# Attention scores as four 64-row products side by side, and a fifth addition of a head's exponentials on GpSimd

## The chip, the cores and the metric

One core of one Trainium2 chip. The metric is the device time of one execution in microseconds (us), lower is better. Engines are named as in the profile: PE (TensorE matmul), PEld (its weight loads), DVE (VectorE), ACT (ScalarE), POOL (GpSimd), SP (the queue that issues most DMAs).

## The reference

A pre-normed transformer layer in float32 on x of 4 batches, 1024 tokens, 128 features: attention with 16 heads of 64, rotary embedding on the first 32 of each head's 64 dimensions, and a low-rank feed-forward part.

```python
x = x + attn(layernorm(x), Wq, Wkv, Wout, bout)
x = x + ffn(layernorm(x), U1, V1, b1, U2, V2, b2)
# attn, per head:
q, k = rope(q), rope(k)
sim = einsum('bhid,bhjd->bhij', q, k) * 64 ** -0.5
out = einsum('bhij,bhjd->bhid', softmax(sim), v)      # then out @ Wout + bout
# ffn:
gelu((x @ U1) @ V1 + b1) @ U2 @ V2 + b2
```

## The kernel before

**Passes and steps.** The 64 (batch, head) pairs are worked in 16 groups of `GH` = 4 heads. The first and the last group are written out, the 14 between are a loop; a group is one pass of `STEPS` = 32 steps. Step t scores one tile of 128 keys (`kt` = t % 8) of head t // 8 against all 1024 queries, in two halves z of 512. Scores lie transposed in `S`, keys on partitions; `S` has a buffer for even and one for odd steps.

**A step.** PE makes the scores (`pe_scores`), ACT writes their exponentials to one of 8 slots of `PF` (`act_step`), PE multiplies them with V into `O` (`pe_values`; at even steps, for steps t-4 and t-3, in float32, the two halves on two 64-column tiles of PE). Queries and keys are kept as float16 high and low parts. In `QK` the 128 partitions hold two 64-row operands each: `KHL` is key-high over key-low, `QHH` query-high twice, `KMH` a constant over key-high, `QML` the row maxima over query-low, so that two products of 128 rows per half (L376, L377) give all three partial products and the subtracted maximum.

**Maxima.** Before a head is scored, "units" estimate each query's maximum: `pe_unit` (L397) makes a 128 x 1024 block of scores in `M` with 64-row operands, two products on the two row halves of PE, and DVE takes the maximum of each row (`dve_max`, L603). Unit u = t + 12 (`LEAD`) is made at step t. `M` is one buffer, so that unit u waits until DVE has read unit u-1. At even steps the unit comes behind the V products, at odd steps at the very end. ACT scales the eight maxima of a head (`act_max`), a DMA lays them down as a row (`max_over`).

**Tiles.** Other work of PE goes through one PSUM bank `TILE`, one tile after another, each at the step that the tables say, behind the scores: 8 projections of q and k for the next group (`QK_AT`; "rot" for the rotated halves, "pass" for the rest), 4 of V (`V_AT`), the sums of the denominators on 128x32 tiles (`DEN_AT`) and the output projections (`OUT_AT`). A tile waits until the one before has been read (`freed`). A rot tile of step s goes to DVE (two operations), to POOL (`rot_add`, L652 and L655), to ACT (`act_rot`, step s+3) and to POOL again (`rot_low`, L663, step s+4), which leaves the low part in `STAGE`. A pass tile is copied by ACT (L433) and subtracted by DVE (L535).

**Handover.** `hand_over` (L708, L709; 4 DMAs a head) carries q and k from `STAGE` to `QK`. For head 0 of the next group it waits until all four rot_low and pass subtractions of the pass are done (`rot_lo`, `pass_lo`); unit 32, at step 20, waits for it (`handed`).

**Sums.** For the denominators POOL adds the exponentials of two steps into `SA[0]` or `SA[1]` (`pool_sum`, L676): parts 0 to 3 of a head at POOL steps 8h+2, 8h+4, 8h+6, 8h+8. DVE adds these four into `SUM` with three additions (`dve_sum`, L610 at `kt` 7, L613 at `kt` 1 and 3 of the next head). POOL's part 2 waits for the first of them, parts 0 and 1 of the next head for the others. Denominators are inverted (`INVERT_AT`), spread by DMA, and DVE scales the outputs by them (`dve_norm`, L625, `NORM_AT`).

Every engine works its own steps in order; what stands in front on an engine holds up what is behind it.

Of the kernel before, what the change touches and what calls it, by code (L numbers as in the profile page):

```python
# [27 lines left out]
HAND = 4 * 16  # L28
PV_LAG = 4
# [76 lines left out]
def build(nc, x_d, wq_d, wkv_d, wout_d, bout_d, u1_d, v1_d, b1_d, u2_d, v2_d, b2_d, rope_d, ident_d, out_d):  # L106
    with ExitStack() as ctx:
# [38 lines left out]
        HIGH, LOW = {"k": STAGE[:, 1], "q": STAGE[:, 2]}, {"k": STAGE[:, 0], "q": STAGE[:, 3]}  # L146
# [12 lines left out]
        MX = sb("MX", [P, 2, KT], F32)  # L159
        MN = sb("MN", [P, 2, KT], F16)  # L160
# [9 lines left out]
        H = [QK[:, h, :, :].rearrange("p a b -> p (a b)").bitcast(F32) for h in range(2)]  # L170
        QT = QK[:, 3, :, :].rearrange("p a b -> p (a b)").bitcast(F32)
# [69 lines left out]


# [150 lines left out]
        def pe_unit(e, u, place, q, bank):  # L393

            for c in range(2):
                rows, keys = slice(DH * c, DH * c + DH), slice(c * 512, (c + 1) * 512)
                mm = e.matmul(bank[:, keys], QHH[rows, place, q:N:KT], (KHL, KMH)[c][rows, place, keys],  # L397
                              start=True, stop=True)
            mm.then_inc(unit_made, 1)
# [9 lines left out]
        def pe_step(e, it, t):  # L409
            u = t + LEAD  # L410
            if t % 2 == 0:
                for back in (t - PV_LAG, t - PV_LAG + 1):
                    if back >= 0:
                        pe_values(e, it.step(back), it.i * GH + back // KT, back, it.i)
                    elif not it.first:
                        pe_values(e, it.step(back), it.i * GH - 1, back + STEPS, it.i - 1)
                if not (it.last and u >= STEPS):
                    pe_next_unit(e, it, u)
            pe_scores(e, it, t)
            pe_tiles(e, it, t)  # L420
            if t % 2 == 1 and not (it.last and u >= STEPS):
                pe_next_unit(e, it, u)


        def act_tile(e, kind, args, made, g, bank):

            if kind == "proj" and args[2] == "pass":
# [5 lines left out]
                e.activation(HIGH[w][:, 1, c * 512:(c + 1) * 512], bank, ACT.Copy).then_inc(pass_hi, 1)  # L433
# [9 lines left out]
        def act_rot(e, args, g):  # L443
# [7 lines left out]
            e.activation(HIGH[w][:, 0, c * 512:(c + 1) * 512], YR[:, :], ACT.Copy).then_inc(rot_hi, 1)  # L451
# [21 lines left out]
        def act_tiles(e, it, t):  # L473
            for n, kind, args in it.at(t):
# [7 lines left out]
                elif kind == "den":  # L482
                    act_den(e, it.pair(args), made, bank)
# [626 lines left out]
```

## Time and profile before

| | |
|---|---|
| median of 3 runs | 1556.92 us (1556.63 to 1557.19) |
| the profiled execution: time / span | 1557.27 us / 1555.5 us |
| PE busy | 1424.9 us, 92% |
| DVE busy | 1222.0 us, 79% |
| POOL busy | 977.8 us, 63% |
| ACT busy | 778.3 us, 50% |
| PEld busy | 546.8 us, 35% |
| chain of waits that ended last | PE 56%, DVE 13%, issue 13%, POOL 7%, DMA 5% |
| granted TensorE clock, mean | 0.986 |

The span is the profiler's, from the first to the last instruction; the execution's own time is 1.8 us more. Busy times are sums over the instructions of an engine, matmuls that run side by side counted once. Clock is the share of full speed that PE was granted. In the timelines a line stands for consecutive instructions of one kind: it gives their start, their length together and, in brackets, the idle time before and what ended it. A matmul's line reaches to its modelled end, so the next one can start before it.

### The profile page before, as it was taken

To read this page: it belongs to the slowest core of one execution; us is meant where nothing else is said; L and a number is where in the kernel's file an instruction comes from. 1 tells how busy PE (TensorE), PEld (TensorE's weight loads), DVE (VectorE), ACT (ScalarE), POOL (GpSimd) and SP (SyncE) were. 2 spreads that over 40 slices of the span, in tenths; PEclk is the share of its full clock that TensorE was granted. 3 is DMA by queue.
4 is the path that set the end of the run, shared out by engine and by line. 5 is a ranking of instruction groups with operands and counts; after the bars stand their busy time and mean duration, and the time that the engine had idled before them with its cause. 6 is when DMAs were issued, how large, how long until landed. Compare 5 with 4: busy or idle time off the path is not lost.

```text
span 1555.5 us, 25971 instructions
## 1 busy us (share of the span) xinstructions
PE 1424.9 (92%) x7289; PEld 546.8 (35%) x7289; DVE 1222.0 (79%) x1297; ACT 778.3 (50%) x1512; POOL 977.8 (63%) x501
## 2 busy tenths in 40 slices
PE   3689999999999999999999999999999999998886
PEld 1224333333333333333333333333333333333323
DVE  7787888788788878878788888878887887888744
ACT  3244554545454545555455454545545554544464
POOL 4388766658475665838476574848566584757731
PEclk9799999999999999999999999999999999999999
DMA  5312131221303121120313122031312204031002
GB/s 158 73 26 60 25 76 26 50 54 26 83 14 75 34 57 38 44 65 14 75 34 74 22 54 54 14 79 30 75 21 54 54 20 89 14 75 33 3 15 68
DMA packets 70209, 76.00 MB, mean 49 GB/s; under 512 B 27204, under 2 KB 36936, under 8 KB 69928
## 3 DMA queue, kind: packets, MB, share of 16 engines
q1 hardware_dynamic: 68736, 74.69, 21.4%
q10 hardware_dynamic: 1448, 1.00, 0.3%
q8 instruction: 13, 0.21, 0.1%
q14 instruction: 12, 0.10, 0.0%
HBM read 22.56 MB, written 2.36 MB: 16 GB/s over the span
## 4 chain that ended last, share of the span: by engine, by line
PE 56%; DVE 13%; issue 13%; POOL 7%; DMA 5%; ACT 3%; SPq 2%; DVEq 0%; ACTq 0%; POOLq 0%
PE O L388 18%; PE S L376 10%; PE S L377 8%; PE M L397 8%; DVE MX L603 5%; PE TILE L312 5%; DVE SUM L613 4%; DMA QK<-STAGE 4%; POOL SA L676 3%; PE TILE L322 2%; POOL STAGE L663 2%; ACT PF L515 2%; SPq L708 1%; PE TILE L306 1%; PE TILE L330 1%
## 5 line engine op out<-in xcount | busy, mean ns | idle before, releaser
L676 POOL TENSOR_TENSOR SA<-PF 128x1024 f32<-128x1024 f32 x256 | 616.5, 2424 | 372.5 <-DVE SUM L610 279.9
L515 ACT ACTIVATE PF<-S 128x512 f32<-128x512 f32 x1024 | 547.8, 599 | 564.9 <-PE S L377 564.1
L603 DVE TENSOR_REDUCE MX<-M 128x1 f32<-128x1024 f32 x504 | 614.5, 1219 | 229.3 <-PE M L397 229.1
L388 PE MATMUL O<-PF,V 128*64 128x512 f32 x2048 | 497.4, 607 | 0.0
L376 PE MATMUL S<-QK 128*128 128x512 f16 x1024 | 393.1, 384 | 0.0
L377 PE MATMUL S<-QK 128*128 128x512 f16 x1024 | 390.1, 381 | 0.0
L397 PE MATMUL M<-QK 64*128 64x512 f16 x1008 | 221.9, 437 | 65.9 <-DVE MX L603 47.7
L613 DVE TENSOR_TENSOR SUM<-SUM,SA 128x1024 f32<-128x1024 f32 x128 | 248.3, 1939 | 3.6 <-POOL SA L676 3.4
L397 PEld LDWEIGHTS M<-QK 64*128 64x128 f16 x1008 | 72.6, 140 | 370.8 <-DVE MX L603 247.9
L388 PEld LDWEIGHTS O<-PF,V 128*64 128x64 f32 x2048 | 124.5, 136 | 206.4 <-issue 149.8
L376 PEld LDWEIGHTS S<-QK 128*128 128x128 f16 x1024 | 99.9, 98 | 165.3 <-issue 64.2
L652 POOL TENSOR_TENSOR T<-T,ROPE 128x512 f32<-128x512 f32 x60 | 76.3, 1271 | 127.8 <-DVE T L532 127.8
L494 ACT ACTIVATE OS<-O 64x512 f32<-64x512 f32 x128 | 75.8, 592 | 130.8 <-PE O L388 130.0
L377 PEld LDWEIGHTS S<-QK 128*128 128x128 f16 x1024 | 100.7, 98 | 76.8 <-issue 1.4
L655 POOL TENSOR_TENSOR YR<-T 128x512 f32<-128x512 f32 x60 | 113.1, 1886 | 4.7
L663 POOL TENSOR_TENSOR STAGE<-YR,STAGE 128x512 f16<-128x512 f32 x64 | 97.7, 1526 | 21.1 <-ACT STAGE L451 21.1
L312 PE MATMUL TILE<-XT,WQK 128*128 (+1 forms) x372 | 102.4, 385 | 6.3 <-ACT V L441 2.6
L610 DVE TENSOR_TENSOR SUM<-SA 128x1024 f32<-128x1024 f32 x64 | 81.8, 1278 | 19.8 <-ACT DS L471 19.8
L330 PE MATMUL TILE<-WO,OS 128*128 (+1 forms) x504 | 68.9, 280 | 16.9 <-DVE OS L625 14.7
L625 DVE TENSOR_TENSOR OS<-OS,RB 128x1024 f32<-128x1024 f32 x32 | 78.7, 2460 | 6.4 <-DMA RB<-den 6.4
L330 PEld LDWEIGHTS TILE<-WO,OS 128*128 128x128 f32 x504 | 65.6, 194 | 31.5 <-issue 21.7
L539 DVE TENSOR_TENSOR X<-TILE,X 128x512 f32 (+1 forms) x63 | 43.2, 685 | 29.4 <-PE TILE L330 29.4
(96 smaller groups left out, 749.0 us busy)
## 6 DMA issues: line engine op xcount, KB each, us to landing
QK<-STAGE SPq DMA_DIRECT2D x128, 256.0 KB, 3.9
QK<-STAGE SPq DMA_DIRECT2D x128, 128.0 KB, 3.1
RB<-den SPq DMA_DIRECT2D x128, 128.0 KB, 3.0
X<-in_L_attn_queries SPq DMA_DIRECT2D x4, 512.0 KB, 12.8
RT<-DS SPq DMA_DIRECT2D x128, 2.0 KB, 1.7
out<-X SPq DMA_DIRECT2D x8, 256.0 KB, 2.3
WRAW<-in_L_attn_Wkv SPq DMA_DIRECT2D x1, 1024.0 KB, 8.7
ROPE<-in_rope SPq DMA_DIRECT2D x1, 1024.0 KB, 12.0
```

The lines of the kernel that those rows point to most:

```text
L312: mm = e.matmul(bank, WQK[:, "qk".index(w), wp, kind, cols], XT[:, xp, rows], start=(n == 0), stop=(n == 2))
L330: mm = e.matmul(bank[:, j * P:(j + 1) * P], OS[:, parity, z, j * P:(j + 1) * P], WO[:, pair, :], start=True, stop=True)
L376: e.matmul(S[:, t % 2, rows], KHL[:, h, keys], QHH[:, h, rows], start=True, stop=False)
L377: e.matmul(S[:, t % 2, rows], KMH[:, h, keys], QML[:, h, rows], start=False, stop=True).then_inc(scored, 1)
L388: mm = e.matmul(O[DH * z:DH * z + DH, :], V[:, h, kt * DH:(kt + 1) * DH], PF[:, t % SLOTS, z * HALF:(z + 1) * HALF], start=(kt == 0), stop ...
L397: mm = e.matmul(bank[:, keys], QHH[rows, place, q:N:KT], (KHL, KMH)[c][rows, place, keys], start=True, stop=True)
L515: e.activation(PF[:, t % SLOTS, z * HALF:(z + 1) * HALF], S[:, t % 2, z * HALF:(z + 1) * HALF], ACT.Exp, scale=EXP_SCALE).then_inc(exped, 1)
L603: e.tensor_reduce(MX[:, place % 2, q:q + 1], bank, AX, ALU.max).then_inc(max_read, 1)
L613: e.tensor_tensor(SUM[:, h % 2, :], SUM[:, h % 2, :], SA[:, part - 1, :], ALU.add).then_inc(summed, 1)
L655: e.tensor_tensor(YR[:, :], T1[:, :], T2[:, :], ALU.add).then_inc(rot_sum, 1)
L663: e.tensor_tensor(LOW[w][:, 0, cols], YR[:, :], HIGH[w][:, 0, cols], ALU.subtract).then_inc(rot_lo, 1)
L676: e.tensor_tensor(SA[:, (t // 2) % 2, :], PF[:, t % SLOTS, :], PF[:, t % SLOTS + 1, :], ALU.add).then_inc(two_summed, 1)
```

## The change

- **Scores.** `QK` holds three 64-row operands per half of the partitions. The queries of half z = 0 lie on partitions 0 to 63, those of z = 1 on 64 to 127, keys on both. `pe_scores` makes four products per half, each on 64 rows (high x high, high x low, low x high, constant x maxima), the halves in turn on the two row halves of PE: eight instructions of 512 columns where there were four. The maxima are in a tile `MQ` of their own, and only the last product waits for them.
- **Units** take 128 queries and 1024 keys as before, from the new layout; DVE takes two maxima per row (`MXP`) and a small `dve_merge` joins them per head.
- **Order on PE.** A tile of an even step stands between the V products and the unit, one of an odd step behind the unit, last in the step. The unit of an odd step stands right behind the scores. ACT works an even tile before its exponentials; DVE takes its maximum first in a step, and a tile in the tile's own step.
- **Order on POOL.** In a step the sum comes first, then rot_low, then rot_add. Behind part 3 POOL adds `SA[1]` to `SA[0]` (`pool_join`), and DVE makes two additions per head: at `kt` 7, and at `kt` 2 of the next head, which waits for the join.
- **DMAs.** A handover has four DMAs of 3 x 1024 elements on 32 partitions each (before 2 x 1024 and 4 x 1024), the maxima of a head two DMAs (before one). POOL's opening memsets are of `MQ` and `MSC`.
- The step tables change as below.

```diff
-QK_AT = (1, 3, 5, 7, 9, 11, 13, 15)
-V_AT = {8: (1, 0), 10: (1, 1), 22: (0, 0), 24: (0, 1)}
-DEN_AT = {6: 1, 20: 0}
+QK_AT = (0, 2, 4, 7, 9, 11, 13, 15)
+V_AT = {17: (1, 0), 18: (1, 1), 24: (0, 0), 26: (0, 1)}
+DEN_AT = {6: 1, 22: 0}
 INVERT_AT = {9: 1, 23: 0}
-NORM_AT = {16: 1, 26: 0}
-OUT_AT = {17: (1, 0), 19: (1, 1), 28: (0, 0), 30: (0, 1)}
-SUM_AT = {7: 0, 1: 1, 3: 2}
+NORM_AT = {15: 1, 27: 0}
+OUT_AT = {19: (1, 0), 21: (1, 1), 29: (0, 0), 31: (0, 1)}
+SUM_AT = {7: 0, 2: 1}
...
+            for z in range(2):
+                wait(e, exped, 2 * n + z - 3)
+                e.matmul(S[:, t % 2, z * HALF:(z + 1) * HALF], KH[z][:, h, keys], QH[z][:, h, :],
+                         start=True, stop=False)
+            for z in range(2):
+                e.matmul(S[:, t % 2, z * HALF:(z + 1) * HALF], KH[z][:, h, keys], QL[z][:, h, :],
+                         start=False, stop=False)
+            for z in range(2):
+                e.matmul(S[:, t % 2, z * HALF:(z + 1) * HALF], KL[z][:, h, keys], QH[z][:, h, :],
+                         start=False, stop=False)
             if kt == 0:
...
             for z in range(2):
...
+                side = slice(DH * z, DH * z + DH)
+                e.matmul(S[:, t % 2, z * HALF:(z + 1) * HALF], MSC[side, :], MQ[side, h, :],
                          start=False, stop=True).then_inc(scored, 1)
...
         def dve_sum(e, head, h, part):
 
-            e.wait_ge(two_summed, head * (KT // 2) + part + 2)
             if part == 0:
+                e.wait_ge(two_summed, head * (KT // 2) + 2)
...
             else:
-                e.wait_ge(summed, 3 * head + part)
-                e.tensor_tensor(SUM[:, h % 2, :], SUM[:, h % 2, :], SA[:, part - 1, :], ALU.add).then_inc(summed, 1)
+                e.wait_ge(four_summed, head + 1)
+                e.wait_ge(summed, 2 * head + 1)
+                e.tensor_tensor(SUM[:, h % 2, :], SUM[:, h % 2, :], SA[:, 0, :], ALU.add).then_inc(summed, 1)
...
         def pool_step(e, it, t):
+            if t % 2 == 0 and (not it.first or t > 0):
+                back = t - 2
+                head, part = it.i * GH + back // KT, (back % KT) // 2
+                pool_sum(e, back % STEPS, it.i * (STEPS // 2) + back // 2, 2 * head + (0, 0, 1, 1)[part])
+                if part == 3:
+                    pool_join(e, it.i * (STEPS // 2) + back // 2, head)
             for n, kind, args in it.at(t - 4):
                 if kind == "proj" and args[2] == "rot":
                     rot_low(e, args, it.i + 1)
             for n, kind, args in it.at(t - 1):
                 if kind == "proj" and args[2] == "rot":
                     rot_add(e, args, it.i + 1)
-            if t % 2 == 0 and (not it.first or t > 0):
-                back = t - 2
-                head, part = it.i * GH + back // KT, (back % KT) // 2
-                pool_sum(e, back % STEPS, it.i * (STEPS // 2) + back // 2, 3 * head + (-1, 0, 1, 1)[part])
```

**The order on POOL around steps 14 to 17 of a pass.** Before, the last rot_add (L652, L655) stands ahead of parts 2 and 3 of head 1 (L676), and rot_low (L663) behind them:

```order
L652 TENSOR_TENSOR T<-T,ROPE 128x512 [waits rot_read]
L655 TENSOR_TENSOR YR<-T 128x512 [waits rot_lo,rot_parts]
L674 ISA
L212 REGISTER_ALU [waits exped]
L676 TENSOR_TENSOR SA<-PF 128x1024 [waits summed]
L674 ISA
L676 TENSOR_TENSOR SA<-PF 128x1024 [waits summed,exped]
L663 TENSOR_TENSOR STAGE<-YR,STAGE 128x512 [waits rot_hi]
```

Now part 2 (L715) stands first, then rot_add (L692, L695), part 3, the join (L721) and rot_low (L702):

```order
L217 REGISTER_ALU [waits exped]
L715 TENSOR_TENSOR SA<-PF 128x1024 [waits summed]
L691 REGISTER_ALU
L692 TENSOR_TENSOR T<-T,ROPE 128x512 [waits rot_read]
L695 TENSOR_TENSOR YR<-T 128x512 [waits rot_lo,rot_parts]
L713 ISA
L715 TENSOR_TENSOR SA<-PF 128x1024 [waits summed,exped]
L720 REGISTER_ALU
L721 TENSOR_TENSOR SA<-SA 128x1024 [waits two_summed]
L702 TENSOR_TENSOR STAGE<-YR,STAGE 128x512 [waits rot_hi]
```

rot_add has moved behind an addition that waits for DVE (`summed`), and between it and rot_low there are two additions of 128x1024, one of them new.

**The order on DVE at steps 14 to 16.** Before, the first addition of head 1 (L610) comes between the maxima of steps 14 and 15, the pass subtraction (L535) and the norm (L625) after that of step 15:

```order
L603 TENSOR_REDUCE MX<-M 128x1 [waits unit_made]
L607 ISA
L212 REGISTER_ALU [waits two_summed]
L610 TENSOR_TENSOR SUM<-SA 128x1024 [waits den_copied]
L600 REGISTER_ALU
L603 TENSOR_REDUCE MX<-M 128x1 [waits unit_made]
L534 REGISTER_ALU
L535 TENSOR_TENSOR STAGE<-TILE,STAGE 128x512 [waits pass_hi]
L624 ISA [waits spread_in]
L625 TENSOR_TENSOR OS<-OS,RB 128x1024 [waits o_copied]
```

Now all three stand between the maximum of step 15 and that of step 16 (L633):

```order
L633 TENSOR_REDUCE MXP<-M 128x2 [waits unit_made]
L564 REGISTER_ALU
L565 TENSOR_TENSOR STAGE<-TILE,STAGE 128x512 [waits pass_hi]
L645 ISA
L217 REGISTER_ALU [waits two_summed]
L647 TENSOR_TENSOR SUM<-SA 128x1024 [waits den_copied]
L662 ISA [waits spread_in]
L663 TENSOR_TENSOR OS<-OS,RB 128x1024 [waits o_copied]
L630 REGISTER_ALU
L633 TENSOR_REDUCE MXP<-M 128x2 [waits unit_made]
```

The addition (L647) stands behind the subtraction, which waits for ACT's copy of the pass tile (`pass_hi`).

## Rows read from the trace of the kernel before

**Rows 1.** The page, part 1: engine, busy us (share of the span), instructions.

```profile
PE 1424.9 (92%) x7289; PEld 546.8 (35%) x7289; DVE 1222.0 (79%) x1297; ACT 778.3 (50%) x1512; POOL 977.8 (63%) x501
```

**Rows 2.** A middle pass by stretch: length, PE, PEld, DVE, ACT, POOL busy, clock.

```profile
601.50:691.00 89.50, 85.49 (x442) 32.58 (x440) 72.51 (x69) 45.93 (x90) 57.11 (x29) 1.00 0.21 47
```

**Rows 3.** Who waited for whom: us in total, times, longest.

```profile
POOL SA L676 <- DVE SUM L610: 279.9, 48, 8.9
...
PE M L397 <- DMA QK<-STAGE: 17.0, 16, 6.5
```

**Rows 4.** Timeline, steps 12 to 14: start us, us, engine, line, operation, count.

```profile
634.69 1.94 PE L388 MATMUL O<-PF,V 128*64 128x512 f32 x8
...
636.56 0.44 PE L397 MATMUL M<-QK 64*128 64x512 f16 x2
...
636.92 0.39 PE L376 MATMUL S<-QK 128*128 128x512 f16 x1
...
637.15 0.38 PE L377 MATMUL S<-QK 128*128 128x512 f16 x1
...
637.64 1.09 ACT L515 ACTIVATE PF<-S 128x512 f32<-128x512 f32 x2 [2.63 <-PE S L377]
...
638.66 0.81 PE L312 MATMUL TILE<-XT,WQK 128*128 x3
...
639.40 0.44 PE L397 MATMUL M<-QK 64*128 64x512 f16 x2
...
639.77 0.65 PE L388 MATMUL O<-PF,V 128*64 128x512 f32 x2
```

**Rows 5.** Timeline of PE's weight loads, the same scores.

```profile
637.15 0.10 PEld L376 LDWEIGHTS S<-QK 128*128 128x128 f16 x1
```

**Rows 6.** Timeline of ACT, steps 14 and 15.

```profile
642.73 2.07 ACT L515 ACTIVATE PF<-S 128x512 f32<-128x512 f32 x4 [2.41 <-PE S L377]
644.66 0.63 ACT L433 ACTIVATE STAGE<-TILE 128x512 f16<-128x512 f32 x1
```

**Rows 7.** Timeline of DVE, steps 15 and 16.

```profile
643.38 1.41 DVE L610 TENSOR_TENSOR SUM<-SA 128x1024 f32<-128x1024 f32 x1
...
646.11 0.68 DVE L535 TENSOR_TENSOR STAGE<-TILE,STAGE 128x512 f16<-128x512 f32 x1
646.71 2.60 DVE L625 TENSOR_TENSOR OS<-OS,RB 128x1024 f32<-128x1024 f32 x1
```

**Rows 8.** Timeline of GpSimd (POOL): first a quiet stretch, then steps 13 to 17.

```profile
622.97 4.67 POOL L676 TENSOR_TENSOR SA<-PF 128x1024 f32<-128x1024 f32 x2 [1.16 <-DVE SUM L610]
...
639.33 1.16 POOL L663 TENSOR_TENSOR STAGE<-YR,STAGE 128x512 f16<-128x512 f32 x1
642.44 1.27 POOL L652 TENSOR_TENSOR T<-T,ROPE 128x512 f32<-128x512 f32 x1 [1.95 <-DVE T L532]
643.78 2.13 POOL L655 TENSOR_TENSOR YR<-T 128x512 f32<-128x512 f32 x1
645.87 5.64 POOL L676 TENSOR_TENSOR SA<-PF 128x1024 f32<-128x1024 f32 x2
651.48 2.14 POOL L663 TENSOR_TENSOR STAGE<-YR,STAGE 128x512 f16<-128x512 f32 x1
```

**Rows 9.** Timeline of the DMA queue on SP after step 17.

```profile
653.73 0.70 SPq L708 DMA_DIRECT2D QK<-STAGE  x1
```

**Rows 10.** Timeline of PE: the unit of step 20 that waits for the handover.

```profile
659.74 0.44 PE L397 MATMUL M<-QK 64*128 64x512 f16 x2 [0.55 <-DMA QK<-STAGE]
```

**Rows 11.** Timeline of PE, first pass: the same wait, longer.

```profile
116.23 0.65 PE L397 MATMUL M<-QK 64*128 64x512 f16 x2 [2.91 <-DMA QK<-STAGE]
```

**Rows 12.** Busy time and granted clock around it (columns as in Rows 2).

```profile
112.00:116.00 4.00, 1.32 (x8) 0.15 (x4) 1.47 (x2) 0.00 (x0) 4.00 (x3) 0.94 0.96 198
116.00:118.00 2.00, 1.77 (x5) 0.58 (x6) 1.08 (x1) 0.12 (x1) 1.92 (x3) 0.50 0.96 192
...
120.00:122.00 2.00, 2.00 (x8) 0.66 (x5) 0.00 (x0) 1.12 (x3) 2.00 (x2) 0.50 0.00 0
```

More of the change, by code:

```diff
@@ L28 @@
 HAND = 4 * 16
+ROWS = 2 * 16
 PV_LAG = 4
@@ L393, in pe_unit @@
         def pe_unit(e, u, place, q, bank):
[L395 to L398, printed above, removed]
+            part, half = q // 2, q % 2
+            for z in range(2):
+                mm = e.matmul(bank[:, z * HALF:(z + 1) * HALF], QH[z][:, place, part:HALF:KT // 2],
+                              KH[z][:, place, half * 512:(half + 1) * 512], start=True, stop=True)
             mm.then_inc(unit_made, 1)
@@ L416, in pe_step @@
                         pe_values(e, it.step(back), it.i * GH - 1, back + STEPS, it.i - 1)
+                pe_tiles(e, it, t)
                 if not (it.last and u >= STEPS):
                     pe_next_unit(e, it, u)
[L419 to L422, printed above, removed]
+                pe_scores(e, it, t)
+            else:
+                pe_scores(e, it, t)
+                if not (it.last and u >= STEPS):
+                    pe_next_unit(e, it, u)
+                pe_tiles(e, it, t)
         def act_tile(e, kind, args, made, g, bank):
@@ L497, in act_max @@
         def act_max(e, head, place):
-            e.wait_ge(max_read, KT * (head + 1))
-            wait(e, max_row, 16 * (head - 1))
-            e.activation(MN[:, place % 2, :], MX[:, place % 2, :], ACT.Copy, scale=-1.0 / MSCALE).then_inc(max_found, 1)
+            e.wait_ge(max_merged, head + 1)
+            wait(e, max_row, ROWS * (head - 1))
+            e.activation(MN[:, place % 2, :, :], MX[:, place % 2, :, :], ACT.Copy,
+                         scale=-1.0 / MSCALE).then_inc(max_found, 1)
         def act_step(e, it, t):
@@ L541, in dve_tiles @@
         def dve_tiles(e, it, t):
-            for n, kind, args in it.at(t - 1):
+            for n, kind, args in it.at(t):
                 made, bank = it.tile0 + n + 1, T[:, :]
@@ L629, in dve_step @@
             h, kt = t // KT, t % KT
+            if not (it.last and u >= STEPS):
+                dve_max(e, it.step(u), it.i * GH + u // KT, (u // KT) % GH, u % KT, M[:, :])
+            if u % KT == 0 and not (it.last and u > STEPS):
+                dve_merge(e, it.i * GH + u // KT - 1, (u // KT - 1) % GH)
             dve_tiles(e, it, t)
@@ L642, in dve_step @@
                 dve_norm(e, it.pair(NORM_AT[t]), NORM_AT[t])
-            if not (it.last and u >= STEPS):
-                dve_max(e, it.step(u), it.i * GH + u // KT, (u // KT) % GH, u % KT, M[:, :])
         def rot_add(e, args, g):
@@ L714, in max_over @@
             wait(sp, scored, head * 16 - 48)
-            row = QML[0:1, place, :].rearrange("o (p t) -> o p t", t=KT)
-            sp.dma_start(row, MN[:, place % 2, :]).then_inc(max_row, 16)
+            for z in range(2):
+                row = MQ[DH * z:DH * z + 1, place, :].rearrange("o (p t) -> o p t", t=KT // 2)
+                sp.dma_start(row, MN[:, place % 2, z, :]).then_inc(max_row, 16)
         def den_over(sp, what, q):
@@ L1046, in _ @@
             loop(dve, body)
-            for part in (1, 2):
-                dve_sum(dve, GROUPS * GH - 1, GH - 1, part)
+            dve_sum(dve, GROUPS * GH - 1, GH - 1, 1)
             def result(c):
```

98 lines of the change are left out of this document (60 added, 38 removed).

## The prediction

> **What bounds the kernel now.** I read the page first: PE is busy for 1424.9 of 1555.5 us, DVE for 1222.0, POOL for 977.8 [rows 1]. That is an average, so next a middle pass: 89.5 us long, PE idle for 4.0 of them, DVE for 17, POOL for 32, clock at full speed [rows 2]. So PE sets the pace, and its small gaps tell what else binds. The waits name it [rows 3]: POOL's additions idle 279.9 us for DVE's first addition of a head, which costs nothing while POOL has slack; but PE waits 16 times for the handover DMA, once a pass. So the chain POOL, SP queue, handover is already in time only just: in the pass shown PE idles 0.55 us at the unit of step 20 [rows 10].
>
> **PE's own work.** From starts in [rows 4]: V products to unit 1.87 us, unit to scores 0.36, eight score products 1.74 (0.2175 each, a slot of 512 columns), a q/k tile to the next unit 0.74, unit to V 0.37: 5.08 us for two steps. Streaming alone is 1.72 + 1.74 + 0.43 (two units, a slot each, since the two row halves run side by side) + 0.65 = 4.54. The rest, 0.54, lies at four changes between full-array, row-half and column-half products, 0.09 to 0.16 each. The change makes eight score products on row halves in place of four on all rows: side by side, four slots again, 0.87 us a step, so nothing there. Units and scores are then of one kind, so two changes of four go from each pair of steps (16 x 0.26 = 4.2 us a pass), but each of 18 tiles now stands between unlike neighbours and brings one (18 x 0.1 = 1.8). Net 2.4 us a pass, some 37 us in all, if nothing waits.
>
> A price is missing: no row shows row-half pairs following each other without a break. Bounds are nothing (the pair of a unit takes one slot) and 0.10 us a slot, a whole weight load uncovered. I take nothing. The nearest row is the load of the next score product, which starts at 637.15, together with a product on the same rows, and leaves the spacing at 0.2175 [rows 4, 5]. The Trainium skill (TensorE: Matmul & The Clock Gate, section Part 3: Packing small matmuls) says that a weight load overlaps running products only if their row groups differ. By that rule every slot here would already be longer by a load; these rows disagree.
>
> **DVE and POOL.** DVE loses one 128x1024 addition per head and gets a merge of 128x8. That is 64 x about 1.9 us, but DVE is not what bounds a pass on average; where its work stands matters more, below. POOL gets 64 joins of 2.34 us, the price of an undisturbed sum (two in 4.67, [rows 8]), 9.3 us a pass out of 32 idle. That too would fit on average. The chain to the handover decides. I walk it with the V products of step 14 as zero.
>
> - PE: unit of step 14 at 1.87, scores from 2.1, those of step 15 from 2.95.
> - ACT begins 0.49 us after the last product that it needs starts (637.15 to 637.64, [rows 4]); that product is now the fourth slot, so at 2.1 + 0.65 + 0.49 = 3.2. Exponentials of both steps 2.07 to 5.3, copy of the pass tile 0.6 to 5.9 [rows 6].
> - DVE: the subtraction of step 15 waits for that copy, 0.68, to 6.6; behind it the first addition of head 1, 1.3, to 7.9 [rows 7]. Before, this addition stood ahead of that wait and was done at 644.8, that is at 5.0.
> - POOL: part 2 waits for it, 2.34 to 10.3. Then rot_add, 1.27 + 2.13, to 13.7; part 3 to 16.0; join to 18.4; rot_low, 1.16 alone and 2.14 beside a DVE addition [rows 8], here beside one: 20.1 with 1.7.
> - Handover: before, rot_low ended at 653.62, the queue issued from 653.73, and the unit could start at 659.74: 6.1 us [rows 8 to 10]. Four DMAs and the same bytes now, so 6.1 again: **26.2**.
>
> Before, the same way from 639.77 to 659.74 took 20.0. PE could be there at 17.5 by its prices, or about 21.5 with the waits that the same stretch now gets: the norm (2.6, [rows 7]) has moved ahead of the maximum of step 16, so unit 17 waits some 2.8 us for `M`; and ACT sits in act_rot of step 16 until rot_add is done at 13.7, which holds the exponentials of step 17, the copy of V tile 17, and by it the V tile of step 18. Both are covered by the handover, which then costs PE 4 to 5 us in one piece. So this stretch is 6.2 us longer.
>
> The rest of the pass was 69.5 us. It gains 2.0 by fewer changes. It loses by waits that I find in the same way: the second addition of step 10 waits for the join (part 2, part 3, join: 7.0 after the first addition) and delays units 11 to 12, about 1.7 with ACT's wait for rot_add; the inverse at step 23 comes one step behind its denominator tile, not three, and waits for the DMA of the sums, 0.8; then the addition of step 26 and the norm of step 27 stand close and hold units 28 and 29, 3.0. That is 5.5, against about 2.0 of idle in that part before (4.0 of [rows 2] less 2.0 in the stretch above): +3.5 - 2.0 = +1.5. Between a bare +1.5 and nothing, if these small waits overlap, I take +0.4, since DVE's additions are nearer 1.2 than 1.9 when POOL is in a wait of its own.
>
> **Sum.** +6.6 us a pass, for the 15 passes that hand over: +99. In the last pass POOL stands on the path and gets joins (two or three, 2.34 each), in the first it is loaded with layer-norm work and gets some too: +10. On the profiled execution's 1557.27 us that is 1666; its median of runs is 0.35 lower, so **1665 us**. Ends of the unknowns: rot_low and rot_add undisturbed (1.16, 1.27) and no extra waits elsewhere give +4 a pass, 1620 or a little under; part 2 slowed beside the norm (5.64 for two against 4.67, [rows 8]) and all 1.5 give +9, 1700. So 1600 to 1705 for this case.
>
> **Rivals.**
> - *The clock falls at each handover.* In the first pass PE waited 2.91 us for the same DMA [rows 11]. The granted clock, 0.94 over the four microseconds before, was then 0.50 (1.2 GHz) until 122 [rows 12]: six microseconds at half speed, 3 us of work lost. A wait of 4 to 5 us in every pass invites that. It adds up to 15 x 3 = 45: about 1710. For it: the wait is longer than the one seen. Against: PE is nearly full until it begins, while in rows 12 it was two thirds idle. Chance 0.20.
> - *Faster: POOL keeps up, PE's savings show.* This needs the handover before about 19.5 on the scale above, so that unit 20 does not wait. It would be so if DVE's addition of step 15 or POOL's additions came some 6 us earlier than I find, say if my order of waits on POOL is wrong. Then a pass loses 2.4 us and keeps its waits: 1557 - 15 x 2.4 = 1521, or near 1500 if DVE's lighter load closes gaps. For it: DVE and POOL both have idle time, on average. Against: each term above is a row, and the order on both engines is plain. Chance 0.13.
> - *A smaller loss.* The chain comes out 2 us shorter and DVE's relief pays for the new waits: +1 to +3 a pass, 1557 to 1600. Chance 0.12.
> - *Row halves do not hide their weight loads.* 4 slots x 512 steps x 0.10 = +205, less the 37 and less what the waits cover: about 1720 to 1750. This is what the rule quoted above would give if it held for row halves only. Chance 0.05.
>
> **Numbers.** The case of the sum has 0.50. A measurement of this kernel tells about 0.2%, 3 us, from no change. Slower by more: 0.50 + 0.20 + 0.05 and 0.09 of the small loss, 0.84; same 0.03; faster 0.13. The range reaches from 1565 to 1720: it takes in the sum's case, the clock's and most of the small loss, and leaves out the faster case and the weight loads.
>
> **What would show it.** Right: in a middle pass (about 96 us) PE idles 4 to 5 us at the unit of step 20 for the handover; POOL's rot_low of step 17 ends about 20 us after the V products of step 14, with two sums, the join and rot_add in a row ahead of it; DVE's addition of step 15 ends near 8; the score products of a step start 0.87 us before the next step's; PE's busy time falls by 30 to 40 us. Wrong: a score step of over 1.0 us (weight loads), a granted clock under 1.00 in middle passes (the clock's case), or a unit of step 20 that does not wait (faster).

## The result and the profile after

The changed kernel takes 1677.8 us (median of 4 runs, 1669.32 to 1681.94) against 1557.06 us before: ratio 1.0766, 95% interval 1.0723 to 1.0809. The profiled execution took 1669.32 us with a span of 1667.4 us, 112 us more than the one before. It is the shortest of the four; the granted clock was 0.963 in it and 0.957 to 0.961 in the others.

The page, part 1 and the clock by slices, which answer to [rows 1]:

```profile
PE 1430.4 (86%) x9337; PEld 549.6 (33%) x9337; DVE 1116.1 (67%) x1297; ACT 787.5 (47%) x1512; POOL 1072.6 (64%) x566
...
PEclk9789999999999999999999999999999999999998
```

DVE lost 106 us and POOL gained 95. The 64 joins alone take 150.5 us of POOL; its other work became shorter, rot_add and rot_low above all (L695 and L702 took 163 us, L655 and L663 before 211). PE's busy time did not fall, because part of it ran at half clock. Busy time by engine in two stretches of 95 us, the length of the shortest pass (columns as in [rows 2]):

```profile
601.00:696.00 95.00, 83.58 (x558) 31.80 (x554) 65.31 (x68) 45.81 (x89) 62.50 (x33) 0.98 0.20 45
...
791.00:886.00 95.00, 85.49 (x559) 32.55 (x557) 66.25 (x68) 43.74 (x86) 61.10 (x32) 0.96 0.21 45
```

The shortest passes are 95 us where they were 89.5, and PE is idle for 9.5 to 11.4 us in such a stretch, before 4.0. The waits (columns as in [rows 3]):

```profile
POOL SA L715 <- DVE SUM L647: 431.4, 64, 16.0
...
PE M L417 <- DVE MXP L633: 88.1, 95, 1.6
...
PE M L417 <- DMA QK<-STAGE: 46.5, 16, 6.7
PE TILE L317 <- ACT V L464: 36.4, 15, 3.0
```

The handover now costs PE 46.5 us in place of 17.0; 6.7 of them, before 6.5, lie at the very first one, near the start. Two further waits are large: units for DVE, and the V tile of step 18 for ACT.

**The stretch that the prediction walked.** PE in the pass with its V products of step 14 at 679.12:

```profile
679.12 1.94 PE L408 MATMUL O<-PF,V 128*64 128x512 f32 x8
680.99 0.41 PE L417 MATMUL M<-QK 64*128 64x512 f16 x2
681.24 0.38 PE L385 MATMUL S<-QK 64*128 64x512 f16 x2
...
682.97 0.38 PE L417 MATMUL M<-QK 64*128 64x512 f16 x2
683.27 0.82 PE L323 MATMUL TILE<-XT,WQK 128*128 x3
684.03 0.65 PE L408 MATMUL O<-PF,V 128*64 128x512 f32 x2
```

POOL's timeline in the same pass:

```profile
686.87 3.26 POOL L715 TENSOR_TENSOR SA<-PF 128x1024 f32<-128x1024 f32 x1 [3.53 <-DVE SUM L647]
690.09 1.26 POOL L692 TENSOR_TENSOR T<-T,ROPE 128x512 f32<-128x512 f32 x1
691.43 1.27 POOL L695 TENSOR_TENSOR YR<-T 128x512 f32<-128x512 f32 x1
692.66 2.34 POOL L715 TENSOR_TENSOR SA<-PF 128x1024 f32<-128x1024 f32 x1
695.08 2.35 POOL L721 TENSOR_TENSOR SA<-SA 128x1024 f32<-128x1024 f32 x1
697.39 1.15 POOL L702 TENSOR_TENSOR STAGE<-YR,STAGE 128x512 f16<-128x512 f32 x1
```

DVE's timeline there:

```profile
684.97 0.69 DVE L565 TENSOR_TENSOR STAGE<-TILE,STAGE 128x512 f16<-128x512 f32 x1 [0.36 <-ACT STAGE L456]
685.58 1.22 DVE L647 TENSOR_TENSOR SUM<-SA 128x1024 f32<-128x1024 f32 x1
686.71 1.22 DVE L663 TENSOR_TENSOR OS<-OS,RB 128x1024 f32<-128x1024 f32 x1
```

ACT's timeline there:

```profile
682.38 2.07 ACT L543 ACTIVATE PF<-S 128x512 f32<-128x512 f32 x4 [0.74 <-PE S L397]
684.30 0.63 ACT L456 ACTIVATE STAGE<-TILE 128x512 f16<-128x512 f32 x1
...
692.73 0.63 ACT L474 ACTIVATE STAGE<-YR 128x512 f16<-128x512 f32 x1 [4.36 <-POOL YR L695]
...
694.23 0.60 ACT L464 ACTIVATE V<-TILE 128x512 f32<-128x512 f32 x1
```

and PE up to the unit of step 20:

```profile
690.63 1.94 PE L408 MATMUL O<-PF,V 128*64 128x512 f32 x8
694.97 1.13 PE L317 MATMUL TILE<-WV,XT 128*128 x12 [2.39 <-ACT V L464]
...
697.07 0.64 PE L391 MATMUL S<-QK 64*128 64x512 f16 x2
697.50 0.64 PE L397 MATMUL S<-MQ,MSC 64*128 64x512 f16 x2
...
704.66 0.41 PE L417 MATMUL M<-QK 64*128 64x512 f16 x2 [1.65 <-DMA QK<-STAGE]
```

| us after the V products of step 14 | predicted | measured |
|---|---|---|
| ACT begins the exponentials of step 14 | 3.2 | 3.3 |
| DVE ends the first addition of head 1 | 7.9 | 7.7 |
| POOL ends part 2 | 10.3 | 11.0 |
| POOL ends rot_add | 13.7 | 13.6 |
| POOL ends part 3 | 16.0 | 15.9 |
| POOL ends the join | 18.4 | 18.3 |
| POOL ends rot_low | 20.1 | 19.4 |
| unit of step 20 | 26.2 | 25.5 |

Before, that unit stood at 20.0 [rows 4, 10]. The unit of step 20 of the following passes starts at 799.76, 897.61 and 994.39: passes of 95.1, 97.9 and 96.8 us. From the second pass on the mean is 96.2 (from 225.23 to 1475.77 in 13 passes), against 89.6 before: +6.6.

### The profile page after: what moved, and what is told of

Its sections match the earlier page's. It is cut to its first block, busy times and chain, and to the rows that moved or that the text cites. A ratio compares the mean times of both kernels' runs of the same rounds, so it can differ in the third digit from the quotient of the medians.

```text
span 1667.4 us, 30140 instructions
## 1 busy us (share of the span) xinstructions
PE 1430.4 (86%) x9337; PEld 549.6 (33%) x9337; DVE 1116.1 (67%) x1297; ACT 787.5 (47%) x1512; POOL 1072.6 (64%) x566
## 4 chain that ended last, share of the span: by engine, by line
issue 35%; POOL 26%; PE 18%; DVE 10%; DMA 5%; ACT 3%; SPq 2%; POOLq 1%; ACTq 0%; DVEq 0%
POOL SA L715 13%; POOL SA L721 5%; DVE MXP L633 5%; PE O L408 4%; DMA QK<-STAGE 4%; POOL STAGE L702 3%; ACT PF L543 3%; POOL T L692 2%; PE M L417 2%; PE S L385 2%; PE S L388 2%; PE S L397 2%; PE S L391 2%; SPq L754 1%; PE TILE L341 1%
## 5 line engine op out<-in xcount | busy, mean ns | idle before, releaser
L715 POOL TENSOR_TENSOR SA<-PF 128x1024 f32<-128x1024 f32 x256 | 626.8, 2463 | 490.5 <-DVE SUM L647 431.4
L633 DVE TENSOR_REDUCE MXP<-M 128x2 f32<-128x1024 f32 x504 | 615.7, 1222 | 389.0 <-PE M L417 387.4
L417 PE MATMUL M<-QK 64*128 64x512 f16 x1008 | 206.4, 405 | 134.9 <-DVE MXP L633 88.1
L385 PE MATMUL S<-QK 64*128 64x512 f16 x1024 | 204.1, 393 | 0.3 <-ACT PF L543 0.2
L391 PE MATMUL S<-QK 64*128 64x512 f16 x1024 | 203.7, 393 | 0.0
L388 PE MATMUL S<-QK 64*128 64x512 f16 x1024 | 203.7, 392 | 0.0
L397 PE MATMUL S<-MQ,MSC 64*128 64x512 f16 x1024 | 202.4, 390 | 0.0
L721 POOL TENSOR_TENSOR SA<-SA 128x1024 f32<-128x1024 f32 x64 | 150.5, 2352 | 5.0
L651 DVE TENSOR_TENSOR SUM<-SUM,SA 128x1024 f32<-128x1024 f32 x64 | 110.8, 1731 | 62.0 <-POOL SA L721 62.0
L317 PE MATMUL TILE<-WV,XT 128*128 (+1 forms) x756 | 63.7, 225 | 36.8 <-ACT V L464 36.4
L474 ACT ACTIVATE STAGE<-YR 128x512 f16<-128x512 f32 x64 | 41.0, 640 | 114.3 <-POOL YR L695 110.8
L695 POOL TENSOR_TENSOR YR<-T 128x512 f32<-128x512 f32 x60 | 88.0, 1467 | 4.7
L692 POOL TENSOR_TENSOR T<-T,ROPE 128x512 f32<-128x512 f32 x60 | 76.1, 1269 | 18.9 <-DVE T L562 18.9
L702 POOL TENSOR_TENSOR STAGE<-YR,STAGE 128x512 f16<-128x512 f32 x64 | 74.6, 1166 | 17.3 <-ACT STAGE L474 17.3
L647 DVE TENSOR_TENSOR SUM<-SA 128x1024 f32<-128x1024 f32 x64 | 77.8, 1216 | 0.0
```

The costliest lines, as they stand in the source:

```text
L385: e.matmul(S[:, t % 2, z * HALF:(z + 1) * HALF], KH[z][:, h, keys], QH[z][:, h, :], start=True, stop=False)
L388: e.matmul(S[:, t % 2, z * HALF:(z + 1) * HALF], KH[z][:, h, keys], QL[z][:, h, :], start=False, stop=False)
L391: e.matmul(S[:, t % 2, z * HALF:(z + 1) * HALF], KL[z][:, h, keys], QH[z][:, h, :], start=False, stop=False)
L397: e.matmul(S[:, t % 2, z * HALF:(z + 1) * HALF], MSC[side, :], MQ[side, h, :], start=False, stop=True).then_inc(scored, 1)
L417: mm = e.matmul(bank[:, z * HALF:(z + 1) * HALF], QH[z][:, place, part:HALF:KT // 2], KH[z][:, place, half * 512:(half + 1) * 512], start= ...
L633: e.tensor_reduce(MXP[:, place % 2, q % 2, :, q // 2], bank.rearrange("p (z n) -> p z n", z=2), AX, ALU.max).then_inc(max_read, 1)
```

## Experiments

Pass lengths below are taken from one denominator tile of step 6 to the next one in the middle of the program; two figures mean that passes differ. "Changed" is the changed kernel: 1677.8 us, passes of 95.1 to 97.9. Before: 1557 us, 89.6. The traces are of the profiled executions, which for the changed kernel is the 1669.3 us one, so that a gain over 1677.8 can be up to 8.5 us more than the traces account for. "Waits for DVE" are those of PE's units for DVE's maxima. A fall of the clock is a stretch at 1.2 GHz, in most places of 3 to 4 us; PE's work in it takes up to 1.7 us longer.

**e1: POOL's old order.** POOL works rot_low and rot_add ahead of the sum.

```diff
         def pool_step(e, it, t):
-            if t % 2 == 0 and (not it.first or t > 0):
-                back = t - 2
...
                     rot_add(e, args, it.i + 1)
+            if t % 2 == 0 and (not it.first or t > 0):
+                back = t - 2
...
```

> The changed kernel with one edit: in a POOL step rot_low and rot_add stand ahead of the sum again, as in the kernel before. Theory (POOL's order up to the handover sets the pass): with the V products of step 14 as zero, rot_add no longer lies between parts 2 and 3, so rot_low ends near 16.0 instead of 19.4 and the unit of step 20 starts near 22.1 instead of 25.5, 3.4 us less a pass, some 50 us in all: about 1620, or 1600 if the clock no longer falls. Rival (DVE's order, with the norm ahead of the maximum of step 16, sets the pass): the unit of step 17 waits as before and less than 10 us are gained, above 1660. Rival (the row-half products cost the time): nothing changes.

Measured: 1663.4 us, ratio 1.067 (1.065 to 1.069), passes of 95.4 to 97.7. A miss for the theory as I had put it. POOL and PE around the handover, V products of step 14 at 487.12:

```profile
494.86 5.58 POOL L715 TENSOR_TENSOR SA<-PF 128x1024 f32<-128x1024 f32 x2 [2.54 <-DVE SUM L647]
500.52 2.35 POOL L721 TENSOR_TENSOR SA<-SA 128x1024 f32<-128x1024 f32 x1
502.83 1.16 POOL L702 TENSOR_TENSOR STAGE<-YR,STAGE 128x512 f16<-128x512 f32 x1
```

```profile
510.19 0.62 PE L417 MATMUL M<-QK 64*128 64x512 f16 x2 [3.61 <-DMA QK<-STAGE]
```

rot_low ended at 16.9 and the unit stood at 23.1: 2.4 us were gained here, of 3.4. But PE's waits for DVE rose from 77.5 to 94.8 us in the middle passes, as rot_low of step 8 now stands ahead of part 3 and of the join that DVE's addition of step 10 waits for (unit 12 waits 2.7 us, in the changed kernel 1.5). And the wait at the handover is now one piece of 3.6 us in every pass: the V tile of step 18 no longer waits, while unit 17 still waits 1.1. Behind the handover the clock is at half in all 13 middle passes (the unit takes 0.62), in the changed kernel in seven of 13. So 2.4 us gained at the handover, 1.2 lost at unit 12 and up to 1.7 lost to the clock leave the shortest pass where it was. POOL's order is one term of several.

**e2: the join undone.**

```diff
-SUM_AT = {7: 0, 2: 1}
+SUM_AT = {7: 0, 1: 1, 3: 2}
...
-                if part == 3:
-                    pool_join(e, it.i * (STEPS // 2) + back // 2, head)
...
-                e.wait_ge(four_summed, head + 1)
+                e.wait_ge(two_summed, head * (KT // 2) + part + 2)
...
```

> The changed kernel with POOL's join taken back: POOL makes four additions of a head, DVE three (at kt 7, 1 and 3). Theory (POOL's chain): rot_low and the handover come 2.35 us earlier, and the second addition of DVE no longer waits for a join: 2.4 to 3.5 us less a pass, 1615 to 1635. Rival (DVE's load sets the pass): DVE gets 64 additions of 1.2 to 1.9 us back, so no gain or a loss, 1670 to 1700.

Measured: 1625.7 us, ratio 1.044 (1.043 to 1.046), passes of 93.4 to 94.8. As the theory said: 52 us less, and the wait for the handover falls from 34.8 us to 2.8 behind the first pass. What is left there is ACT in act_rot: the V tile of step 18 waits 3.2 us in each pass. The edit also frees DVE's second addition from the join; what each of the two gives was not split.

**e3: DVE's first addition ahead of the tile.**

```diff
+            if kt in SUM_AT and SUM_AT[kt] == 0:
+                dve_sum(e, it.i * GH + h, h, 0)
             dve_tiles(e, it, t)
...
-            if kt in SUM_AT and SUM_AT[kt] == 0:
-                dve_sum(e, it.i * GH + h, h, 0)
...
```

> The changed kernel with DVE's first addition of a head (kt 7) ahead of the tile of the same step, so that it doesn't wait for ACT's copy of the pass tile. Theory (POOL's part 2 waits for it, and the handover for POOL): it ends near 6.6 after the V products of step 14 instead of 7.75, the handover comes 1.1 us earlier, 17 us in all and perhaps as much again at steps 7 and 8: 1635 to 1655. Rival (something behind POOL sets the pass): no change, above 1665.

Measured: 1632.6 us, ratio 1.049 (1.047 to 1.050), passes of 93.2 and 94.9. It gains 45 us, a little more than the range said. The edit acts at steps 7 and 15 of a pass; which gives what was not split. Its trace has a fall of the clock about 31 us behind the tile of step 6 in every middle pass, and in the passes of 94.9 a second one behind the handover: that is the difference between its two lengths.

**e4: the join alone, on the kernel before.** The order in POOL's step stays as it was: rotations, then the sum.

```diff
-SUM_AT = {7: 0, 1: 1, 3: 2}
+SUM_AT = {7: 0, 2: 1}
...
+                if part == 3:
+                    pool_join(e, it.i * (STEPS // 2) + back // 2, head)
...
```

> The kernel before with the join alone: POOL makes five of the seven additions, DVE two (at kt 7 and kt 2); scores, tables and orders as before. Theory: the join lies ahead of rot_low of step 17, so the handover is 2.35 us later a pass, and PE waits about 2.9 us at the unit of step 20 instead of 0.55: +35 us, 1592, less up to 10 that DVE's lighter load returns. Rival (the join costs nothing because POOL is idle a third of the time): 1550 to 1557, DVE's relief showing.

Measured: 1603.4 us, ratio 1.030 (1.028 to 1.031), passes of 92.0. So with scores, tables and orders as before, the fifth addition costs 47 us, more than its 35. POOL in that kernel, with V products, scores and tiles where they were:

```profile
667.65 5.64 POOL L677 TENSOR_TENSOR SA<-PF 128x1024 f32<-128x1024 f32 x2
673.37 2.37 POOL L683 TENSOR_TENSOR SA<-SA 128x1024 f32<-128x1024 f32 x1
675.68 1.16 POOL L664 TENSOR_TENSOR STAGE<-YR,STAGE 128x512 f16<-128x512 f32 x1
```

The join stands between part 3 and rot_low. PE waits 1.5 us for the handover, before 0.5 to 0.6, where the theory had 2.9, and 58.3 us for DVE's maxima in the middle passes, before 38.4. So the handover is about 1.0 us a pass of the cost, and the waits for DVE are the larger part, some 20 us in all; DVE's second addition, which waits for the join, is the likely reason, but this was not tried by itself. The 13 middle passes lose 33 us of the 46 between the profiled executions, the passes before and behind them 13.

**e5: the handover's wait filled with products.** On e1: 14 more products of 512 columns ahead of the unit of step 20 in the middle passes, 3.0 us of PE; nothing reads them.

```diff
+                if t == 20 and not it.first and not it.last:
+                    n0 = max(n for n, tile in enumerate(it.tiles) if tile[0] < t)
+                    kind0, args0 = it.tiles[n0][1:]
+                    e.wait_ge(*freed(kind0, args0, it))
+                    for _ in range(14):
+                        e.matmul(T[:, :], WQK[:, 0, 0, 0, 0:P], XT[:, 0, 0:512], start=True, stop=True)
```

> The kernel of e1_rot_first with 14 products of 128x512 float16 more in each of the 14 middle passes, made into the free TILE bank ahead of the unit of step 20; nothing reads them. They take 3.0 us of PE's time in the place where PE waits 3.5 us for the handover. Theory (the wait lets the granted clock fall to half for some 3.4 us behind it, and PE loses 1.7 us each time): the clock stays at full speed through the middle passes and the time falls by 1.5 to 2 us a pass, 20 to 30 us in all, to 1633 to 1643 from 1663. Rival (the clock costs nothing since other waits follow): 1660 or above, since the products only take PE's time.

Measured: 1653.2 us, ratio 1.061 (1.059 to 1.063), against 1663.4 for e1: more work on PE, 10 us less. The wait for the handover is gone in the middle passes (0.2 us in all), and no fall of the clock stands behind it any more. But the clock did not stay at full speed. In 11 of 13 middle passes it falls at another place, behind unit 12, which waits 2.7 us for DVE; in e1 it fell there in only three, with the same wait:

```profile
574.35 0.41 PE L417 MATMUL M<-QK 64*128 64x512 f16 x2 [2.67 <-DVE MXP L639]
```

```profile
576.00:578.00 2.00, 2.00 (x11) 0.46 (x6) 0.61 (x2) 1.89 (x5) 2.00 (x2) 0.50 0.00 0
...
600.00:602.00 2.00, 1.98 (x12) 0.72 (x9) 0.00 (x0) 0.00 (x0) 1.69 (x1) 1.00 0.97 196
```

(Columns as in [rows 2]; the second line is the stretch with the extra products.) Passes with one fall take 95.4 us in both kernels. The two of e5 without a fall take 93.8 and 93.9, so a fall that nothing covers costs some 1.6 us, as the theory said. The 8 us that the 13 passes gain come from these two and from the three of e1 that had two falls. The fill moved the fall more than it removed it, which is why 20 to 30 us did not come; why the clock now falls behind unit 12 was not shown.

**e6: three edits together**: the diffs of e1, e2 and e3.

```diff
-SUM_AT = {7: 0, 2: 1}
+SUM_AT = {7: 0, 1: 1, 3: 2}
...
+            if kt in SUM_AT and SUM_AT[kt] == 0:
+                dve_sum(e, it.i * GH + h, h, 0)
             dve_tiles(e, it, t)
...
```

> The changed kernel with three edits: no join on POOL (four and three additions), rot_low and rot_add ahead of the sum on POOL, the first addition of a head ahead of the tile on DVE. Theory (the chain addition of step 15, part 2, part 3, rot_low, handover): addition done at 6.6, part 2 at 9.0, part 3 at 11.3, rot_low at 12.5, unit of step 20 possible at 18.6 after the V products of step 14, so hardly any wait for the handover; DVE's norm of step 15 still holds unit 17 for some 2.5 us. A pass takes 88 to 90 us: 1545 to 1580. Rival (row-half products or the new place of the units cost time of their own): it stays above 1600.

Measured: 1568.5 us, ratio 1.008 (1.006 to 1.010), passes of 90.2 and 90.8. No middle pass waits for the handover. 109 of the 121 us are back, with row-half products, units and tiles still where the change put them. What holds PE is DVE: 77 us of waits for it, 2.4 of them in each pass at unit 17, behind the norm of step 15.

**e7: norms and inverse later.** On e6:

```diff
-NORM_AT = {15: 1, 27: 0}
+NORM_AT = {16: 1, 28: 0}
-INVERT_AT = {9: 1, 23: 0}
+INVERT_AT = {9: 1, 24: 0}
-OUT_AT = {19: (1, 0), 21: (1, 1), 29: (0, 0), 31: (0, 1)}
+OUT_AT = {19: (1, 0), 21: (1, 1), 30: (0, 0), 31: (0, 1)}
...
-TURN_X0_AT = (21, 23, 25, 27, 28, 30)
+TURN_X0_AT = (21, 23, 25, 27, 28, 29)
```

(The last line moves a transpose of the first pass to step 29, as step 30 now has an output tile.)

> The kernel of e6_three_undone with the norms at steps 16 and 28 in place of 15 and 27 (behind the maximum of an even step), the second inverse at step 24 in place of 23, and the output tiles that need the second norm at steps 30 and 31. Theory (DVE's place of the norms and of the inverse costs units 17, 28 and 29 about 5 us a pass): 2 to 4 us less a pass than e6, 30 to 60 us, so 1500 to 1535, below the kernel before. Rival (these waits only move): within 10 us of e6.

Measured: 1542.3 us, ratio 0.990 (0.988 to 0.991), passes of 88.4, four of 13 of 89.8 to 90.1. PE's waits for DVE fall from 77 to 30 us. Now PE reaches the handover sooner and waits there again:

```profile
565.67 0.41 PE L417 MATMUL M<-QK 64*128 64x512 f16 x2 [2.53 <-DMA QK<-STAGE]
```

So 2.5 us a pass of the gain, 36 in all, turned into the old wait. The clock gives some back: it falls in 12 of 13 middle passes of e6 and in four of e7, at up to 1.7 us each. With the 48 us from DVE these come to about the 26 us measured, an estimate, against the 30 to 60 expected.

**e8: the first norm alone at step 16**, on the changed kernel.

```diff
-NORM_AT = {15: 1, 27: 0}
+NORM_AT = {16: 1, 27: 0}
```

> The changed kernel with the first norm at step 16 in place of 15, nothing else. Theory (that norm holds unit 17, but behind it the handover sets the time, so the wait is covered): less than 10 us gained, 1660 to 1680, while the wait of unit 17 (1.1 us behind a V tile that ACT holds) goes and the wait for the handover grows. Rival (the norm sets the time): 15 x 1.1 to 2.5, 1640 to 1660.

Measured: 1662.1 us, ratio 1.068 (1.066 to 1.069), passes of 95.2 and 96.9. The shortest passes are as long as without the edit (95.1): the wait of unit 17 went, the V tile of step 18 waits 3.6 us for ACT in place of 2.4, and behind it the handover comes at the same time. Its 1662 us lie in the theory's range though the gain, 16 us, is over the 10 it named. Between the profiled executions it is 7.7 us, 6 of them in the 13 middle passes: the clock falls behind the handover in four of them where it did in seven. The rest lies between executions of the changed kernel, of which only one was traced.

**e9: rotations one step sooner.** On e7, act_rot at step s+2 and rot_low at s+3:

```diff
         def act_rots(e, it, t):
-            for n, kind, args in it.at(t - 3):
+            for n, kind, args in it.at(t - 2):
...
-            for n, kind, args in it.at(t - 4):
+            for n, kind, args in it.at(t - 3):
                 if kind == "proj" and args[2] == "rot":
                     rot_low(e, args, it.i + 1)
...
```

> The kernel of e7_norm_later with ACT's act_rot one step sooner (step s+2 of a rot tile of step s) and POOL's rot_low too (step s+3), so that the last rot_low stands ahead of part 3 and not behind it. Theory (the handover still costs 2.5 us in each pass of e7, and what is left is PE's own work): rot_low of the last tile ends some 2.3 us sooner, the unit of step 20 hardly waits, a pass goes from 88.4 us to about 86: 1542 - 15 x 2.4 = 1506. Rival (ACT in act_rot holds exponentials, or DVE's waits take the place): above 1530.

Measured: 1527.6 us, ratio 0.981 (0.979 to 0.983), passes of 87.7. The handover's wait is gone, but the gain is 15 us where 36 were expected: DVE's waits rose from 30 to 53 us. The rival holds in part.

**e10: the same with the join kept**, and DVE's second addition at kt 3.

```diff
-SUM_AT = {7: 0, 1: 1, 3: 2}
+SUM_AT = {7: 0, 3: 1}
...
```

(The lines left out put the join back in behind part 3.)

> As e9_rot_early, but with the join kept (POOL five additions, DVE two, the second at kt 3 in place of 2). The join is behind rot_low here and out of the chain to the handover. Theory (the join costs by its place, not by its length): DVE is lighter by about 7 us a pass, POOL has room, so the same as e9 or faster, 1495 to 1515. Rival (POOL's five additions are too much wherever they stand): 1530 or more.

Measured: 1500.7 us, ratio 0.963 (0.961 to 0.965), passes of 84.6. The page and POOL in steps 14 to 17 (V products of step 14 at 531.38, part 2, rot_low, part 3, join):

```profile
PE 1394.8 (93%) x9337; PEld 532.6 (36%) x9337; DVE 1116.0 (74%) x1297; ACT 793.1 (53%) x1512; POOL 1064.5 (71%) x566
```

```profile
538.69 2.35 POOL L715 TENSOR_TENSOR SA<-PF 128x1024 f32<-128x1024 f32 x1 [1.17 <-DVE SUM L647]
541.00 2.15 POOL L702 TENSOR_TENSOR STAGE<-YR,STAGE 128x512 f16<-128x512 f32 x1
543.10 2.35 POOL L715 TENSOR_TENSOR SA<-PF 128x1024 f32<-128x1024 f32 x1
545.54 2.35 POOL L721 TENSOR_TENSOR SA<-SA 128x1024 f32<-128x1024 f32 x1
```

The same fifth addition now stands behind rot_low, which ends at 11.8 on the prediction's scale. PE's waits for DVE are 14 us in all the middle passes, and the clock falls in none of them, as in e9. This kernel beats both the kernel before and the changed one.

**e11: the join on the kernel before, behind rot_low.** As e4, with the join one step later and DVE's second addition at kt 3.

```diff
-SUM_AT = {7: 0, 2: 1}
+SUM_AT = {7: 0, 3: 1}
...
-                if part == 3:
-                    pool_join(e, it.i * (STEPS // 2) + back // 2, head)
+            if t % 8 == 1 and (not it.first or t > 8):
+                pool_join(e, it.i * (STEPS // 2) + (t - 3) // 2, it.i * GH + (t - 3) // KT)
...
```

> The kernel before with the join, as in e4_before_join, but one step later, behind rot_low, and DVE's second addition at kt 3 in place of 2. Theory (in e4 the join cost 47 us because rot_low and the handover, and DVE's second addition, waited for it): most of that goes, 1555 to 1570. Rival (the fifth addition on POOL costs by its length): 1590 to 1605 as e4.

Measured: 1529.5 us, ratio 0.982 (0.981 to 0.984), passes of 86.6. Not 1555 to 1570: the join in its new place is a gain of 27 us. POOL waits less for DVE's first addition, 208.1 us against 279.9 [rows 3]:

```profile
POOL SA L677 <- DVE SUM L610: 208.1, 47, 7.0
```

and PE waits 8 us for DVE's maxima in the middle passes, before 38. Two things differ from e4, the place of the join and the step of DVE's second addition (kt 3, not 2); the 74 us between the two kernels were not split between them.

## Why the prediction was right

**The chain.** The step that carried it, DVE's addition behind ACT's copy, part 2, rot_add, part 3, join, rot_low, handover, held to 0.7 us at each mark. e2, e3 and e4 each take or put one link of it and move the time the right way by 52, 45 and 47 us. They move it by more than the handover's wait, though: in e4 this wait explains about 1.0 us a pass, and waits for DVE's maxima the larger part. e1, the fourth test of the chain, gained 14 us where 50 were expected.

**Terms that were mis-sized.** The norm was taken at 2.6 us from [rows 7]; it took 1.22, and POOL's part 2 beside it 3.26 in place of 2.34. So unit 17 waited 1.1 and not 2.8, and part 2 ended 0.7 later. rot_add gave that back: it took 1.26 + 1.27, not 1.27 + 2.13, as none of DVE's additions ran beside it. rot_low then took 1.15, not 1.7, and the last marks came 0.7 early. That the errors of part 2 and rot_add cancel is luck. PE therefore waited at the handover for 1.6 to 3.4 us, not 4 to 5 in one piece: the V tile of step 18 had taken 2.4 of it, behind ACT in act_rot, and in the pass shown the scores of steps 18 and 19 ran at half clock, 1.7 us more.

**The rest of the pass.** It was 95.1 - 25.5 = 69.6 us in the shortest passes against 69.5, with +0.4 forecast. The waits found came to +1.5, and 0.4 was a choice between that and nothing, so the match to 0.3 us is partly luck. The small waits were there: 1.5 at unit 12 (1.7 forecast), 0.2 at unit 25 (0.8), 1.3 and 1.4 at units 28 and 29 (3.0 for both).

**PE's own work.** A step's scores take 0.87 us in eight row-half products of 0.2155 a pair, and two steps with a tile 4.91 us (679.12 to 684.03), where the prices gave 5.08 - 0.26 + 0.10 = 4.92. So row halves hide their weight loads, and the rival on them fell. PE's busy time did not fall by 30 to 40 us; that sign failed, since the clock was half for part of it. By the granted clock in stretches of 1 us, half speed lengthened PE's busy time by about 50 us, before by 14. Without that it is 1380 against 1411 us, an estimate, and the fall of 30 is there. e10, where this is 24 us, has 1394.8.

**The clock.** It had a chance of 0.20 as a case of its own and was true in part: 1.2 to 2.8 us in 7 of 13 middle passes, 1.1 on the mean pass of the profiled execution. Where the fall came behind the wait of the V tile, the handover's wait took it up and the pass stayed at 95.1; where it came behind the handover it cost its whole length. The sum left it out, and marks that came 0.7 us early paid for most of it: the mean pass is 5.5 longer up to the unit of step 20, 0.1 longer in the rest and 1.1 by the clock, and the forecast of +6.6 was 6.2 + 0.4. The sum agrees; its terms do so less well, and that is luck. 1666 was worked out for the profiled execution, which took 1669.3. The other three runs were longer and had a lower clock, so the median is 1677.8; no trace of them is there to show where. The term for both ends held: between the units of the first and the last handover 94.7 us were lost in 14 passes, forecast 92.4, and outside them 17.2, forecast 10 and one more pass of 6.6.

**What I had undervalued.** That DVE's lighter load is worth anything. The prediction gave the fifth addition a cost by its place and almost no return. e10 against e9 and e11 against the kernel before show the return once it stands off the chain: 27 us each. The 13 middle passes gain 3 us each, 40 and 38 in all; the passes before and behind them lose 13 and 11 of that, which was not followed up.

## What to carry to other kernels

Here, work moved from a loaded engine to one with a third of its time idle was paid by where it stood in that engine's order, not by its length: the same addition cost 47 us ahead of the operation that a DMA waited for and gained 27 behind it, with DVE's addition that waits for it one step later too. Before such a move, walk one pass from the last mark that is fixed to the wait of the busiest engine, with durations from rows; it takes some ten terms and here came out within 1 us, with two errors that cancelled. And when a long wait is shortened, look at what it covered and what stands behind it: e1 and e7 gained less than expected since other waits grew.

## What the runs showed of the hardware that I had not expected

A wait of 2.4 us on PE in an otherwise dense stretch was followed by half the granted clock. By stretches of 2 us in the changed kernel (columns as in [rows 2]; PE's busy time first, clock third from the end):

```profile
692.00:694.00 2.00, 0.57 (x4) 0.00 (x0) 0.00 (x0) 1.27 (x3) 2.00 (x2) 1.00 0.00 0
694.00:696.00 2.00, 1.03 (x12) 0.84 (x12) 0.00 (x0) 1.97 (x4) 1.92 (x2) 1.00 0.00 0
696.00:698.00 2.00, 2.00 (x14) 0.90 (x14) 1.53 (x2) 0.65 (x2) 2.00 (x2) 0.58 0.00 0
698.00:700.00 2.00, 2.00 (x13) 0.57 (x9) 1.62 (x1) 1.22 (x3) 0.84 (x2) 0.57 0.00 0
700.00:702.00 2.00, 2.00 (x16) 1.31 (x16) 1.85 (x2) 0.96 (x2) 2.00 (x1) 1.00 0.95 192
```

PE was busy for 0.57 and 1.03 us of the first two stretches; in the next two, both filled, the clock was 0.58 and 0.57, and from 700 it was 1.00 again (2.4 GHz). In the next pass the fall came behind the handover:

```profile
796.00:798.00 2.00, 0.42 (x2) 0.00 (x0) 0.45 (x1) 0.00 (x0) 2.00 (x2) 1.00 0.94 194
798.00:800.00 2.00, 0.24 (x2) 0.23 (x4) 0.00 (x0) 0.00 (x0) 1.45 (x1) 0.68 0.97 197
800.00:802.00 2.00, 2.00 (x12) 0.83 (x11) 1.30 (x2) 0.00 (x0) 0.00 (x0) 0.50 0.97 191
802.00:804.00 2.00, 2.00 (x12) 0.50 (x8) 0.00 (x0) 1.36 (x4) 0.00 (x0) 0.50 0.61 120
```

The Trainium skill (TensorE: Matmul & The Clock Gate, section Part 1: The HAM clock gate) says that activity releases the throttle and idleness brings it back; these rows agree. At 1.2 GHz a pair of products takes 0.43 us (697.07 to 697.50, above) in place of 0.2155. The length of a wait alone does not tell whether the clock falls: behind the same 2.7 us at unit 12 it fell in three of 13 middle passes of e1 and in 11 of e5, and behind one of 3.0 us in e4 (the unit at 222.91) it stayed at 1.00. What decides was not shown. Filling a wait with products that nobody needs kept the clock up at that place (e5), yet mostly moved the fall to another.

The second surprise is how DVE and POOL share. In [rows 7, 8] the norm took 2.60 us and the two POOL additions around it 5.64, 0.97 more than the quiet pair. In the changed kernel the norm took 1.22 and POOL's addition beside it 3.26, 0.92 more than a quiet one. POOL loses nearly the same in both; DVE loses more than its own length in the one and nothing in the other. Other DVE operations touch these additions too, so the norm need not be all of it. What decides was not tried.
